# Attention in a macaron block: the scores of a step written together, the squares of its probabilities turned in one run of five banks

## The reference

```python
x = x + 0.5 * ffn(layernorm(x))       # 8 experts, the best 2 of each token
x = x + attn(layernorm(x))
x = x + 0.5 * ffn(layernorm(x))

def attn(x):                           # x: 8 x 512 x 128; 16 heads of 64
    q, k, v = (einsum('ahe,bce->bach', w, x) for w in (W_Q, W_K, W_V))
    scores = einsum('bach,baCh->bacC', k, q)
    p = softmax(where(tril, scores, -1e10) / 8)
    z = einsum('bacC,baCh->bach', p, v)
    return einsum('aeh,bach->bce', W_O, z)
```

## Time and profile before

| | |
|---|---|
| time, median of 3 runs | 1076.81 us |
| lowest and highest of the 3 | 1070.95, 1079.96 us |
| the profiled execution: time | 1078.47 us |
| its span | 1075.8 us, granted TensorE clock 0.981 |
| PE busy | 977.6 us, 91% |
| DVE busy | 841.4 us, 78% |
| ACT busy | 730.2 us, 68% |
| attention, 64 steps | from about 236 to 898 us in the span |

### The profile page before, as it was taken

The page is one execution under the profiler, slowest core; times in us unless marked ns, Lnnn a source line. Parts: engine busy times, 40 slices in busy tenths (PEclk is TensorE's granted clock), DMA queues, the critical chain, the costliest instruction groups (busy, mean ns, idle before and its releaser), DMA issues.

```text
span 1075.8 us, 24556 instructions
## 1 busy us (share of the span) xinstructions
PE 977.6 (91%) x7677; PEld 810.3 (75%) x7677; DVE 841.4 (78%) x3091; ACT 730.2 (68%) x2018; POOL 286.6 (27%) x316
## 2 busy tenths in 40 slices
PE   3567899988999999999999999999999998878994
PEld 2456899876777777777777777777777777768994
DVE  7566788577778788878878878978978888657786
ACT  3334667656877878778778777777777775445672
POOL 3665300223101101321311212210200103555554
PEclk9998999998999999999999999999999999989997
DMA  9234645412112102212112112111111124435576
GB/s 258 79 111 135 204 156 163 148 58 42 30 30 42 36 25 44 38 43 43 35 44 41 36 48 39 38 47 28 44 34 26 43 73 115 127 107 158 174 229 181
DMA packets 90623, 90.23 MB, mean 84 GB/s; under 512 B 30080, under 2 KB 66848, under 8 KB 90496
## 3 DMA queue, kind: packets, MB, share of 16 engines
q1 hardware_dynamic: 77296, 67.79, 22.8%
q0 software_dynamic: 8640, 18.76, 7.3%
q10 hardware_dynamic: 4560, 2.12, 0.7%
HBM read 63.95 MB, written 24.67 MB: 82 GB/s over the span
## 4 chain that ended last, share of the span: by engine, by line
PE 75%; DVE 11%; issue 5%; DMA 3%; another core or an unknown queue 2%; ACT 2%; SPq 1%; POOL 1%; DVEq 0%; ACTq 0%; POOLq 0%
PE psum L1737 12%; PE psum L1767 12%; PE psum L1645 10%; PE psum L1616 7%; PE psum L1614 7%; PE psum L1615 6%; PE psum L1748 6%; PE psum L1752 5%; PE psum L1775 5%; PE psum L1756 2%; PE psum L1623 1%; DVE arena L1350 1%; DVE arena L1369 1%; PE psum L1566 1%
## 5 line engine op out<-in xcount | busy, mean ns | idle before, releaser
L794 ACT ACTIVATE arena<-arena,neg_max 128x512 f32<-128x512 f32 (+3 forms) x512 | 281.0, 551 | 49.6 <-DVE neg_max L1350 44.3
L1350 DVE CUSTOM_DVE_ANT_0 arena<-psum,causal 128x512 f32<-128x512 f32 (+3 forms) x512 | 225.3, 488 | 28.3 <-PE psum L1737 21.9
L752 ACT ACTIVATE arena<-psum,b_t 128x256 f32<-128x256 f32 x312 | 124.1, 477 | 63.2 <-PE psum L1616 43.0
L1645 PE MATMUL psum<-w_sb,arena 128*128 x1248 | 156.9, 279 | 4.6 <-issue 2.2
L1645 PEld LDWEIGHTS psum<-w_sb,arena 128*128 128x128 f32 x1248 | 150.1, 196 | 6.2 <-issue 6.2
L1767 PE MATMUL psum<-arena 128*64 128x512 f32 (+3 forms) x1024 | 152.0, 439 | 0.4 <-DVE arena L1363 0.4
L597 POOL DMA_INDIRECT arena<-y_tiles,y_at x64 | 60.8, 950 | 324.6 <-PE psum L1737 210.0
L578 POOL DMA_INDIRECT x_slots<-xr,slot x64 | 61.9, 967 | 255.6 <-PE psum L1737 212.7
L801 ACT ACTIVATE arena<-psum 128x512 f32<-128x512 f32 x128 | 75.5, 590 | 78.1 <-PE psum L1748 78.1
L1767 PEld LDWEIGHTS psum<-arena 128*64 128x64 f32 x1024 | 68.0, 136 | 77.8 <-issue 59.7
L1363 DVE COPY arena<-psum 128x512 f32<-128x512 f32 x128 | 88.5, 691 | 25.0 <-PE psum L1752 24.1
(11 more groups left out here) (221 smaller groups left out, 2221.6 us busy)
## 6 DMA issues: line engine op xcount, KB each, us to landing
w_raw<-in_L_ffn_W_dram SPq DMA_DIRECT2D x78, 256.0 KB
arena<-inv_dram SPq DMA_DIRECT2D x128, 128.0 KB
xg<-x_slots SPq DMA_DIRECT2D x78, 144.0 KB
y_tiles<-y_sb SPq DMA_DIRECT2D x39, 128.0 KB, 1.7
arena<-y_rows SPq DMA_DIRECT2D x16, 256.0 KB, 3.7
x_slots<-blank SPq DMA_DIRECT2D x18, 144.0 KB
out_dram<-xs ACTq DMA_DIRECT2D x8, 256.0 KB
y_rows<-y_sb,y_tok POOLq DMA_INDIRECT x78
```

The costliest lines, as they stand in the source:

```text
L752: ins = act.activation(h_t[n % 2][:, k, :], H_BANKS[n % 2][k // 2][:, k % 2 * TS:(k % 2 + 1) * TS], ACT.Relu, bias=b1_t[:, bass.ds(e * CHU ...
L794: ins = act.activation(prob_tile(i, h, t), prob_tile(i, h, t), ACT.Exp, scale=-1.0, bias=neg_max[i % 2][:, h, t:t + 1], accum_out=row_sum[ ...
L1350: ins = dve.tensor_tensor_reduce(out=prob_tile(i, h, t), in0=score_tile(t)[:, h, :], in1=causal[:, SEQ - (t + 1) * P:SEQ], scale=-1.0, sca ...
L1645: ins = pe.matmul(Y_BANKS[n % 2][:, r * D:(r + 1) * D], h_t[n % 2][:, k, r * P:(r + 1) * P], w2_sb[:, bass.ds(e * (CHUNKS * D) + k * D, D) ...
```

## The change

All four row tiles of a step are now scored ahead of the turning. Row tiles 0 and 1 go to SIDES (banks 4 and 6, one per head) in place of LONG, so they wait for `z_ready` and for the small job's reader, and no longer for the `maxima` of tile 3. All twenty squares of both heads are then turned in one run, four to a bank, in the banks RING_B, LONG[0], LONG[1], RING_B, LONG[0]. ACT copies groups 0, 2 and 3, DVE groups 1 and 4, each of 512 columns: three copies in place of four on ACT, two of the same size as before on DVE. `project_out` comes ahead of the run. `attend` follows `project_v` (and the small job) directly. DVE takes the `maxima` of tiles 1 and 0 between its two copies, ahead of the side work, and ACT makes all its copies ahead of the exponentials of tile 3. The last step's run uses RING_B, RING_A, RING_C, RING_B, RING_A.

```diff
-        probs_t = [lot(10 * P) for h in range(2)]
+        probs_t = lot(20 * P)
-        S_USES, PT_USES, PT_ACT, PT_DVE, V_PAIRS = 3, 6, 4, 2, 4
+        S_USES, PT_USES, PT_ACT, PT_DVE, V_PAIRS = 3, 5, 3, 2, 4
-        LONG, SHORT = psum[:, 0:2, :], psum[:, 2:4, :]
+        LONG, SHORT, SIDES = bank[0:2], bank[2:4], bank[4:8:2]
-        def score_tile(t):
-            both = (LONG, LONG, SHORT, LONG)[t]
-            col = P if t == 1 else 0
-            return both[:, :, col:col + (t + 1) * P]
+        def score_tile(t, h):
+            both = (SIDES, SIDES, SHORT, LONG)[t]
+            col = 2 * P if t == 0 else 0
+            return both[h][:, col:col + (t + 1) * P]
+        def turned_bank(i, g):
+            if i == STEPS - 1:
+                return (RING_B, RING_A, RING_C, RING_B, RING_A)[g]
+            return (RING_B, LONG[0], LONG[1], RING_B, LONG[0])[g]
...
 # ACT
-            def transposed(i, h):
-                act.wait_ge(pt_ps, PT_USES * i + 3 * h + 1)
+            def transposed(i):
                 wait(act, z_ps, i)
-                act.activation(probs_t[h][:, 0:4 * P], RING_A, ACT.Copy).then_inc(pt_act, 1)
-                act.wait_ge(pt_ps, PT_USES * i + 3 * h + 3)
-                act.activation(probs_t[h][:, 8 * P:10 * P], RING_C[:, 0:2 * P], ACT.Copy).then_inc(pt_act, 1)
+                for g in (0, 2, 3):
+                    act.wait_ge(pt_ps, PT_USES * i + g + 1)
+                    act.activation(four_turned(g), turned_bank(i, g), ACT.Copy).then_inc(pt_act, 1)
                     if i > 0:
-                        transposed(i - 1, 0)
+                        transposed(i - 1)
                     exps(i, 0, [3])
-                    if i > 0:
-                        transposed(i - 1, 1)
...
-                    exps(i, 2, [0, 1])
+                    exps(i, 2, [1, 0])
...
 # DVE
                     maxima(i, 0, [3])
                     if i > 0:
                         invert(i - 1)
-                        transposed(i - 1, 0)
                     maxima(i, 1, [2])
                     if i > 0:
                         transposed(i - 1, 1)
+                    maxima(i, 2, [1, 0])
+                    if i > 0:
+                        transposed(i - 1, 4)
...
                     go_on(work, 2)
-                    maxima(i, 2, [0, 1])
...
 # PE
+            def transposes(i):
+                squares = [(h, k, t) for h in range(2) for k in range(QT) for t in range(k, QT)]
+                for g in range(5):
+                    if i < STEPS - 1 and g == 1:
+                        pe.wait_ge(max_ready, S_USES * (i + 1) + 1)
...
+                    if g == 3:
+                        pe.wait_ge(pt_act, PT_ACT * i + 1)
+                    if g == 4:
+                        pe.wait_ge(pt_dve, PT_DVE * i + 1)
+                    for n, (h, k, t) in enumerate(squares[4 * g:4 * g + 4]):
+                        col = P_COL[t] + k * P
+                        ins = pe.transpose(turned_bank(i, g)[:, n * P:(n + 1) * P], probs[i % 2][h][:, col:col + P], ident[:, :])
+                    ins.then_inc(pt_ps, 1)
...
                     scores(i, 3).then_inc(s_ps, 1)
                     scores(i, 2).then_inc(s_ps, 1)
-                    if i > 0:
-                        pe.wait_ge(v_ready, min(i + QT - 1, STEPS))
+                    if i == 0:
+                        pe.wait_ge(v_ready, QT - 1)
+                    else:
                         ring_a_taken(i - 1)
-                        pe.wait_ge(exp_done, S_USES * i)
                         wait(pe, z_ready, i - 1)
-                        transposes(i - 1, 0)
+                    scores(i, 1)
+                    scores(i, 0).then_inc(s_ps, 1)
                     if i > 1:
                         project_out(i - 2)
                     if i > 0:
-                        transposes(i - 1, 1)
+                        pe.wait_ge(v_ready, min(i + QT - 1, STEPS))
+                        pe.wait_ge(exp_done, S_USES * i)
+                        transposes(i - 1)
...
                     if i + QT - 1 < STEPS:
-                        wait(pe, pt_dve, PT_DVE * i)
+                        wait(pe, pt_act, PT_ACT * i)
...
                     if i > 0:
                         pe.wait_ge(pt_act, PT_ACT * i)
+                    pe.wait_ge(max_ready, S_USES * (i + 1))
...
-                    pe.wait_ge(max_ready, S_USES * i + 1)
-                    scores(i, 0)
-                    scores(i, 1).then_inc(s_ps, 1)
                     if i > 0:
                         attend(i - 1)
...
-                transposes(STEPS - 1, 0)
+                transposes(STEPS - 1)
                 project_out(STEPS - 2)
                 spread_keys(1, AUX)
-                transposes(STEPS - 1, 1)
```

More of the change, by code:

```diff
@@ L1736, in scores @@
                         m = slice(h * DH, (h + 1) * DH)
-                        ins = pe.matmul(score_tile(t)[:, h, :], k[m, tile], q[m, 0:(t + 1) * P], start=(n == 0), stop=(n == 2))
+                        ins = pe.matmul(score_tile(t, h), k[m, tile], q[m, 0:(t + 1) * P], start=(n == 0), stop=(n == 2))
                 return ins
-            def transposes(i, h):
-                src = probs[i % 2][h]
-                def square(k, t):
-                    return src[:, P_COL[t] + k * P:P_COL[t] + (k + 1) * P]
-                wait(pe, pt_act, PT_ACT * i + 1 if h else 0)
-                for t in range(QT):
-                    ins = pe.transpose(RING_A[:, t * P:(t + 1) * P], square(0, t), ident[:, :])
-                ins.then_inc(pt_ps, 1)
-                wait(pe, pt_dve, PT_DVE * i + 1 if h else 0)
-                for n, (k, t) in enumerate(((1, 1), (1, 2), (1, 3), (2, 2))):
-                    ins = pe.transpose(RING_B[:, n * P:(n + 1) * P], square(k, t), ident[:, :])
-                ins.then_inc(pt_ps, 1)
-                wait(pe, pt_act, PT_ACT * i + 2 if h else 0)
-                for n, (k, t) in enumerate(((2, 3), (3, 3))):
-                    ins = pe.transpose(RING_C[:, n * P:(n + 1) * P], square(k, t), ident[:, :])
-                ins.then_inc(pt_ps, 1)
@@ new lines, in ring_a_taken @@
+            def ring_a_taken(i):
+                b, s = divmod(i, PAIRS)
+                if s == TURN_STEP and b + 1 < BATCH:
+                    pe.wait_ge(xn_lo_ready, b + 2)
+                if b > 0 and s == route_step(b):
+                    pe.wait_ge(xt_taken, BATCH + b)
+                if b > 0 and s == route_step(b) + 1:
+                    pe.wait_ge(logits_taken, U1 + b)
+                if counted(i) is not None:
+                    pe.wait_ge(places_taken, U1 + counted(i) + 1)
+                if b == BATCH - 1 and s == KEY_STEP:
+                    pe.wait_ge(there_ready, tables(1, 0))
+                if b == BATCH - 1 and s == ORDER_STEP:
+                    pe.wait_ge(hits_ready, tables(1, 0))
+                if b == BATCH - 1 and s == LIST_STEP:
+                    pe.wait_ge(tabled, tables(1, 0))
@@ new lines, in transposes @@
+            def transposes(i):
[3 more added lines that the diff above has]
+                        pe.wait_ge(max_ready, S_USES * (i + 1) + 1)
+                    if i == STEPS - 1 and g == 1:
+                        ring_a_taken(i)
+                    if i == STEPS - 1 and g == 2:
+                        pe.wait_ge(z_ready, i)
+                    if g == 3:
[6 more added lines that the diff above has]
+                    ins.then_inc(pt_ps, 1)
@@ L1767, in attend @@
                         ins = pe.matmul(RING_C[m, k * P:SEQ], v_sb[i // V_PAIRS % 2][:, k, col:col + DH],
-                                        probs_t[h][:, PT_COL[k]:PT_COL[k] + SEQ - k * P], start=(k == 0), stop=(k == QT - 1))
+                                        probs_t[:, h * 10 * P + PT_COL[k]:h * 10 * P + PT_COL[k] + SEQ - k * P], start=(k == 0), stop=(k == QT - 1))
                 ins.then_inc(z_ps, 1)
@@ L1804, in attention @@
                     b, s = divmod(i, PAIRS)
-                    wait(pe, max_ready, S_USES * i)
                     pe.wait_ge(qk_lo_ready, 2 * (i + 1))
@@ L1835, in attention @@
                         transpose_rows(BATCH + b - 1, rows_of(U1 + b - 1), RING_A)
+                    if b == BATCH - 1 and s == LIST_STEP:
+                        list_tiles(1, 0, RING_A[:, P:])
                     if b > 0 and s == route_step(b) + 1:
```

35 lines of the change are left out of this document (8 added, 27 removed).

## The result

| | before | changed |
|---|---|---|
| median of 4 runs | 1077.0 us | 1089.5 us |
| lowest and highest | 1070.95, 1079.96 | 1086.51, 1091.49 |
| the profiled execution, its span | 1078.47, 1075.8 | 1091.49, 1089.7 |
| PE, DVE, ACT busy | 977.6, 841.4, 730.2 us | 983.4, 829.7, 707.7 us |
| steps 2 to 62 of attention | 621.4 us | 635.3 us |

The changed kernel takes 1.0121 times as long, with a 95% interval of 1.0069 to 1.0173. The forecast was 1079.7, within 1%: the time lies inside the range, yet in the case called slower, and on the wrong side of the likeliest case. ACT and DVE have less work than before, PE the same 7677 instructions; so what is longer is waiting. The 5.8 us that PE is busy for longer are part of it: a weight load that comes late by less than the tail of the matmul ahead of it leaves no idle time on PE, and in step 63 PE runs at a lower clock for a while.

What follows compares the result with a forecast made beforehand. PE was taken to set the pace. Five light steps (-0.25) and three full ones (+0.57) over eight batches gave +2.6 us, plus 0.3 for the last run: +2.9, 1081.4, or 1079.7 against the median; range 1069 to 1091.

Steps and rivals of the forecast that it cites:

- the case called slower: Whole kernel slower by more than about 1%, here 11 us, through DVE or stalled copies; chance 0.22.
- the likeliest case: Whole kernel much as before, lost joint and new waits cancelling; chance 0.64, own range 1072 to 1087.
- The joints: PE's changes of tile shape: three a step instead of four, about 0.15 us each; net minus 0.20 us a step.
- The rival in which the joint wins 0.35 a step: PE in light steps: no price for v to `attend`, no group 4 stall; steps 9.61, total 1068; chance 0.14.
- The stalls on groups 3 and 4: PE's turning waits to reuse the banks of groups 0 and 1: 0.03 and 0.10 us a step.
- the run of squares stalls on its copies: Turning waits for ACT's and DVE's copies when banks are reused: 12 us typically, 22 at most, 1092; chance 0.09.
- 0.04 to start: ACT's copy of group 0 was to start 0.04 us after the group's end at T+0.60.
- +0.57 per batch: DVE's queue in steps 1 to 3 of a batch: together 30.54 us where they take 29.97.
- The forecast's last line: Signs of being wrong: light steps over 0.15 off 9.9, or PE waiting for the divide beyond a batch's first three steps.
- DVE becomes the bound: Full steps cost 0.6 us more than counted as DVE loses cover behind `split_k`: 14 us, 1094; chance 0.13.
- The cover of 0.02 us: Tile 1's scores on PE: load at 1.28 just covers the divide's signal; cost 0 to 0.05 us a step.
- The last run: Last run of squares, without `project_out` and a small job between the heads: costs about 0.3 us.

Runs made afterwards that it cites:

- the profile at 1038 us: The changed kernel run again unedited, on another chip beside the kernel before: 1038.5 us against 1026.9, ratio 1.0112.
- the fill: Changed kernel with two of five pieces of side work ahead of the divide moved into DVE's idle time before its first copy: 1029.1 us, 1.0019 of before.
- one wait moved: Changed kernel with DVE's gap filled, small job's reader wait put ahead of tile 2's scores, ACT's high parts earlier in step 63: 1025.6 us, 0.9990 of before.
- the end in order: The 1025.6 us kernel, with DVE copying group 1 of the last run after four leftover pieces, group 4 after six more: 1084.9 us, 1.0098 of before.

## Why the prediction was right and wrong

**The joints: right, size and place.** `attend` follows v at 0.32 us (313.45 to 313.77 in the light step), as assumed from the other joints; the last pair of scores starts 1.89 us into the step (308.08 against 306.19); light steps are 9.88 and 9.89. The price was 0.15 by reading and is 0.17 by experiment, for changes between 64\*128 and 128\*128; for the change to 128\*64 there is only the start, the same 0.32. The Trainium skill (TensorEngine Tiling (Array Packing), section Tiling Modes, Key Properties) calls for a drain at each change of mode; these rows agree, for the change from 128\*128 to 128\*64 too. The rival in which the joint wins 0.35 a step is thus out.

**The stalls on groups 3 and 4: right where the signals come on time.** 0.04 and 0.06 us against 0.03 and 0.10. The argument against the rival "the run of squares stalls on its copies" was that ACT stands idle before its first copy. It does, for 2.57 us, and its copy is late all the same in some 30 steps. What failed is the time between the last square and the copy: the forecast has "0.04 to start" there, that is, a signal that is raised as the matmul ends. It measures 0.10 where the signal is on time (0.01 for the signal, 0.08 for the start), and up to 0.65 at the level of 1075 us, where the signal comes late. In batches 2 to 5 this makes 334.5 us out of 329.7 in the changed kernel, 0.15 a step, and 7 us over steps 3 to 62 (624.6 and 624.1 against 617.3). The kernel before has late signals too, but none that its copies wait for.

**DVE: the mechanism right, the size short.** Between starts of the divide, steps 1, 2 and 3 of batch 3 take 10.50, 10.11 and 10.30 us in the profile at 1038 us, where no copy is late, together 30.91, where I had 10.41, 9.95 and 10.18, together 30.54, and before has 29.97. The term was +0.57 per batch and is +0.94, some 3 us more over eight batches. The reason is the gap ahead of the first copy, read off the timeline of DVE in step 1:

```profile
468.90 1.08 DVE L1374 TENSOR_TENSOR arena<-psum,arena 128x512 f32<-128x512 f32 x1
...
472.14 0.09 DVE L1355 DVE_READ_ACCUMULATOR2_ANT neg_max<- 128x1 f32 x1
473.04 0.69 DVE L1368 COPY arena<-psum 128x512 f32<-128x512 f32 x1 [0.81 <-PE psum L1780]
...
479.40 1.06 DVE L1374 TENSOR_TENSOR arena<-psum,arena 128x512 f32<-128x512 f32 x1
```

The idle time is 0.81 where I counted 0.52: what lies ahead of it takes 3.33 us, not 3.44, and the copy starts at 4.14 from the divide, not 3.96. Of these 0.18 us, 0.05 are a slip in the sum (T+1.08 is 4.13 in the step, and 4.01 from a divide that starts at 0.12), and the turning itself starts 0.09 later behind a small job. In PE's steps the lateness shows in steps 2, 3 and 4 of a batch (10.38, 10.13, 10.73 against 9.88, 9.88, 10.32 with the fill), 1.16 us a batch, where the forecast's terms make 0.90 (30.54 less three steps of 9.88). The forecast's last line names the first three steps of a batch as those in which PE may wait; the steps that pay are the ones behind steps 1, 2 and 3. The rival "DVE becomes the bound" was nearer to the truth than its 0.13: where it had 14 us, there are 8.1 in steps 3 to 62 and, in the profile at 1038 us, step 2's 3.4.

The forecast also says that PE is busy for all of every window before. In step 2 of the batch it is not: PE is busy for 9.98 of 10.13 us and waits 0.15 for the divide of step 1. So DVE set the pace there already, which is why the fill brings this step 0.26 under before.

```profile
500.74:510.87 10.13, 9.98 (x80) 7.50 (x78) 9.45 (x39) 8.30 (x26) 1.89 (x2) 1.00 0.25 41
```

**The two waits ahead of tile 1: cost 0.02 in the sum, 0.09 measured.** The cover of 0.02 us was reckoned with the divide's signal alone. Where a small job ran, PE takes two waits one behind the other, and with the second gone the step falls from 9.97 to 9.88. I had bounded it at 0.05. In about 30 steps this is 3.0 us.

**The last run: +0.3 in the sum, +2.8 measured in the first profile.** I looked at which work no longer lies between the heads, not at what stands ahead of the two copies in DVE's queue, nor at ACT, whose exponentials of step 63 end later. The reuse of a bank makes the leftover side work a wait of PE: 1.5 us. Behind it the clock fell in the first profile (0.71 over the 5.9 us from 906.1), as in the next one, and with the same waits it didn't in the two others of the changed kernel, whose step 63 takes 20.0. So about 1.3 of the 2.8 us are the waits, and 1.5 are a fall of the clock that comes in some executions only. The first profile:

```profile
902.20:906.10 3.90, 2.10 (x19) 1.63 (x17) 3.45 (x16) 3.26 (x8) 0.97 (x1) 1.00 0.05 5
906.10:912.00 5.90, 5.90 (x33) 4.25 (x34) 2.89 (x10) 0.90 (x2) 3.13 (x3) 0.71 0.68 189
```

With two changes of order, in ACT and in DVE, step 63 takes 18.9 us in all three profiles.

**The start, left out of the sum.** From the first scores to the end of step 2 the changed kernel was 4.2 us shorter than before in the first profile, but 3.5 longer at the level of 1026 (17.55 + 14.03 against 18.13 + 9.93). It differs between executions by as much as most terms of my sum. In step 2 itself most of the difference is the clock, which the two waits of 1.46 and 1.18 us bring down in one profile and a single one of 1.45 does not in another.

Put together: of the forecast's +2.9 us, steps 3 to 62 have about +2.4. At the level of 1026 us these steps take 6.8 more than before (617.3 against 610.5): 4.3 less with the divide on time and one wait moved (606.2), 8.1 for the late divide, 3.0 for the second wait. At the level of the first profile the late signals add about 7, and it has 13.3 over before. To this come the last step (+2.8 and, at 1026, +3.0, where I had 0.3), step 2 (+0.6 and +4.1) and the way to step 2, which I had left out (2.3 earlier in the first profile, 3.4 at 1026). They come to the 13.9 and 10.4 us between the spans within 1 us. The single steps of the reasoning erred by little and all to one side, since each was taken at the low end of what a chain so close to its covers (0.02, 0.05, 0.10 us) can cost; the late signals were in no term at all. That 1089.5 us still lies inside the range is in part luck: the 7 us of the signals and the 1.5 of the clock are nothing that the range was made for, and the earlier start gives 2.3 back.

## What to carry to other kernels

When work is moved up from the end of an in-order queue, what stood ahead of it moves to the end, where the next step's first instruction pays for it, and a gap opens where the moved work now waits: fill that gap with side work in the same edit (9.4 of the 11.6 us here, where the signals were on time). Take the first and the last step of a pipeline as kernels of their own, with their side work; in the last one DVE's copies stood behind 15 pieces. And where a cover is below 0.1 us, count it as a cost: a second semaphore wait alone took 0.09. Where an idle engine seems to start late on ready data, ask when the semaphore was raised before blaming the engine.

## What the runs showed of the hardware

- A change of tile shape on TensorE between 64\*128 and 128\*128 costs 0.17 us (two more in each step: 638.1 against 617.3 us in steps 3 to 62). Where the columns change, from 128\*128 to 128\*64, the next start comes after 0.32 us instead of 0.23, as for the change of rows.
- A second semaphore wait ahead of a matmul, for a signal that has long come, costs TensorE 0.09 us (steps of 9.97 fall to 9.88).
- A semaphore can be raised well behind the end of the instruction that raises it. In the groups of runs where the kernel before takes about 1075 us, PE's signal for group 0 comes 0.11 to 0.58 us late in 28, 31 and 41 of 61 steps of three profiles; where it takes 1026 us, never over 0.02. ACT starts 0.08 us behind it in each. In the steps of batches 2 to 5 in which POOL issues two indirect transfers near 1.25 and 2.5 us, all engines and queues together raise 0.0 to 0.1 semaphores a step between 3.6 and 3.9 us at the slower level, the kernel before included, and 3.5 to 4.2 at the faster one (two profiles), while some 70 to 110 DMA packets start there at either level (about 50 in the profile with the end in order). Before loses little by it, since the signals of its first copies are due at 2.1 us. That POOL's transfers are the cause is argued from their being there in each late step; the kernels that move them never ran where signals are late, so it is open.
- After waits of 1.46 and 1.18 us close behind each other TensorE's granted clock was 1.2 GHz from 231.75 to 238.6 us, though PE was busy again from 232.5 on; after 1.63 and 0.57 us it stayed at 2.4 GHz. After a wait of 1.3 to 1.6 us in the last step it fell for 3.4 us in five profiles, and after waits of 1.5 to 1.6 us in the same place it did not in four others.
- The same kernel took 1077 and 1026 us in different groups of runs, with attention alike within 0.2%: the first scores start at 234.8 us in the one and 215.1 in the other, and what follows attention takes 178.2 and 154.1. The late signals go with the slower level (284 against 5 in the two profiles of the kernel before); that they are what makes it slower isn't shown. The changed kernel's ratio was 1.012, 1.011 and 1.009 all the same, with its loss made up differently.
